# A transformer layer on one core: the last chunk's attention rows divided with features on the partitions

## The reference

```
h = layernorm(x) * (1 + ca) + sa
q, k, v = h Wq.T + bq, h Wk.T + bk, h Wv.T + bv      # 16 heads of 8 features
scores = q k.T / sqrt(8) * exp(-alpha |i - j|)
out = softmax(scores) v                               # the division of this case
x = x + ga * (out Wo.T + bo)
h = layernorm(x) * (1 + cb) + sb
x = x + gb * (shared(h) + sum over the 2 best of 16 experts of p_e * expert_e(h))
```

## Time and profile before

| what | value |
|---|---|
| median of 3 runs | 241.84 us (241.4 to 242.19) |
| the profiled execution | 241.85 us |
| its span, first to last instruction | 240.1 us |
| TensorE busy | 226.1 us, 94% |
| VectorE busy | 190.9 us, 80% |
| GpSimd busy | 190.2 us, 79% |
| ScalarE busy | 163.3 us, 68% |
| first matmul of the expert stage | 156.08 us |

### The profile page before, as it was taken

How to read it: one execution, slowest core, us unless ns; L and a number is a source line. 1 busy time by engine, 2 the same in 40 slices (tenths; PEclk the granted TensorE clock), 3 DMA queues, 4 the chain that set the end, 5 groups by cost and what they waited for, 6 DMA issues and landing times.

```text
span 240.1 us, 5810 instructions
## 1 busy us (share of the span) xinstructions
PE 226.1 (94%) x1830; PEld 167.3 (70%) x1830; DVE 190.9 (80%) x791; ACT 163.3 (68%) x321; POOL 190.2 (79%) x345
## 2 busy tenths in 40 slices
PE   7997999998999998999999899999999999999994
PEld 7775567665567676557677567677888888688882
DVE  3599788896998889999979988468756886976763
ACT  4447867777867799867887678586657658565550
POOL 6489988999999999997999999618486644676661
PEclk9999999999999999999999999999999999999998
DMA  5717814742006632005734450015323340026211
GB/s 140 222 33 175 282 76 96 200 114 79 0 4 141 191 85 72 0 4 127 201 71 139 165 191 3 3 45 147 108 76 125 122 131 3 0 102 197 104 44 44
DMA packets 16302, 24.38 MB, mean 102 GB/s; under 512 B 3280, under 2 KB 5968, under 8 KB 16144
## 3 DMA queue, kind: packets, MB, share of 16 engines
q1 hardware_dynamic: 15840, 24.01, 34.4%
q10 hardware_dynamic: 432, 0.01, 0.1%
HBM read 13.39 MB, written 1.18 MB: 61 GB/s over the span
## 4 chain that ended last, share of the span: by engine, by line
PE 41%; POOL 39%; DVE 12%; ACT 3%; issue 3%; DVEq 0%; ACTq 0%
PE bank L916 41%; POOL sc L298 34%; DVE sc L711 4%; POOL rstd L271 3%; POOL wgu_sb L307 1%; DVE sc L880 1%; DVE attn_t L634 1%; DVE qk L626 1%; DVE qk_st L808 1%; ACT xn L372 1%; POOL nmr L276 1%; DVE mx L711 1%; POOL nmean L269 1%; ACT L575 1%; DVE cw L703 1%
## 5 line engine op out<-in xcount | busy, mean ns | idle before, releaser
L298 POOL TENSOR_SCALAR sc<-sc,mx 128x256 f32<-128x256 f32 x256 | 122.2, 495 | 4.2 <-DVE mx L711 4.1
L711 DVE CUSTOM_DVE_ANT_0 sc<-bank,decay 128x256 f32<-128x256 f32 x256 | 91.0, 418 | 13.6 <-PE bank L916 13.4
L405 ACT ACTIVATE pr<-bank 128x512 f32<-128x512 f32 x128 | 69.4, 595 | 23.2 <-PE bank L916 23.1
L916 PE MATMUL bank<-id_f,sc 128*128 128x128 f32 x512 | 69.9, 278 | 4.0 <-ACT pr L405 1.9
L347 POOL TENSOR_TENSOR act_lo<-sc,act_hi 128x512 fp32r<-128x512 f32 x35 | 45.2, 1296 | 33.0 <-ACT act_hi L566 33.0
L916 PEld LDWEIGHTS bank<-id_f,sc 128*128 128x128 f32 x512 | 55.8, 141 | 18.7 <-issue 8.7
L916 PE MATMUL bank<-pr,v_one 128*32 128x256 f32 x512 | 34.3, 385 | 0.0
L874 DVE TENSOR_TENSOR pr<-bank,cwb 128x512 f32<-128x512 f32 x32 | 22.0, 687 | 14.3 <-PE bank L916 14.0
L575 ACT ACTIVATE bank<-bank 128x512 f32<-128x512 f32 x32 | 18.6, 582 | 19.0 <-PE bank L916 18.7
L880 DVE TENSOR_TENSOR sc<-pr,bank 128x512 f32<-128x512 f32 x36 | 24.7, 687 | 5.8 <-ACT bank L575 2.6
L916 PE MATMUL bank<-h_hi,wgu_hi 128*128 128x512 f32 x72 | 28.5, 395 | 0.0
(11 more groups left out here) (108 smaller groups left out, 274.9 us busy)
## 6 DMA issues: line engine op xcount, KB each, us to landing
cwb<-cw_dram SPq DMA_DIRECT2D x64, 128.0 KB, 3.0
qk_st<-qk SPq DMA_DIRECT2D x60, 128.0 KB, 2.7
wgu_sb<-in_w_gu SPq DMA_DIRECT2D x1, 1152.0 KB, 5.6
wgu_sb<-in_x_t SPq DMA_DIRECT2D x4, 256.0 KB, 3.5
x_all<-in_x SPq DMA_DIRECT2D x1, 768.0 KB, 6.9
o_sum<-o_t SPq DMA_DIRECT2D x6, 128.0 KB, 2.3
o_val<-o_t SPq DMA_DIRECT2D x6, 128.0 KB, 2.2
out_dram<-wgu_sb SPq DMA_DIRECT2D x3, 256.0 KB, 3.3
```

The source lines that it names most:

```text
L298: last = nc.gpsimd.tensor_scalar(sc[:, n % RING, t, :], sc[:, n % RING, t, :], -1.0, mx[:, n % RING, t:t + 1], ALU.mult, ALU.add)
L405: nc.scalar.activation(pr[:, n % RING, :, :].rearrange("p a b -> p (a b)"), turn_bank(i, n)[:], ACT.Exp, scale=-1.0).then_inc(s["exp_done" ...
L711: last = nc.vector.tensor_tensor_reduce(sc[:, n % RING, t, :], ps_s[n % SB][:, t * SEQ:t * SEQ + SEQ], decay[:, t, :], float(HD) ** -0.5, ...
L916: return nc.tensor.matmul(o, l, r, start=start, stop=stop, skip_group_check=not check, is_transpose=transpose or None)
```

## The change

Chunk 3 is divided as chunks 0 to 2 are: `move_rows(3, k)` on SyncE, behind `weights_out(1)`, and one multiply `norm(3)`. The inverse is taken not by ScalarE's Ln and Exp, but by VectorE's reciprocal on o_sum in place, in four pieces of 128 x 128, between units 2, 3 (two pieces) and 4. `by_token`, `norm_tokens`, `attn_turn` and `attn_take` go. The steps behind the division move: `project_o` and `residual` from u = 4 to 5, `res_turn` and `x2_take` from 5 to 6, the statistics from 6 to 7, the root from behind the split of 7 to that of 8; `weights_turn(2)` goes ahead, from 6 to 3.

```diff
@@ SyncE
             weights_out(1)
+            for k in range(2):
+                move_rows(NCHUNK - 1, k)
@@ GpSimd
-                    if i == 0 and u == 7:
+                    if i == 0 and u == 8:
                         ln2_root(NCHUNK - 1)
                         ln2_shift(NCHUNK - 1)
@@ ScalarE
-                        if u == 3:
-                            attn_take(c)
-                        if u == 5:
+                            weights_take(c - 1)
+                        if u == 6:
                             x2_take(c)
-                        if u == 6:
-                            weights_take(c - 1)
@@ VectorE
-            def norm_tokens(k):
...
+            def inverse_piece(t):
+                if t == 0:
+                    for k in range(2):
+                        dve.wait_ge(s_sums[k], 16 * NCHUNK)
+                at = slice(t * P, t * P + P)
+                last = nc.vector.reciprocal(o_sum[:, at], o_sum[:, at])
+                if t == TT - 1:
+                    last.then_inc(s["rec_ok"], 1)
...
-                    if q == 6:
-                        norm_tokens(0)
...
-                        if u == 1:
-                            norm_tokens(1)
+                        for t in {2: (0,), 3: (1, 2), 4: (3,)}.get(u, ()):
+                            inverse_piece(t)
                         if u == 4:
+                            norm(c)
+                        if u == 5:
                             residual(c)
-                        if u == 6:
+                        if u == 7:
                             dve.wait_ge(s["x2_ok"], c + 1)
@@ TensorE
-                        pe.wait_ge(s["cwt_ok"], i - 1)
-                        by_token(i, 0)
...
-                        pe.wait_ge(s["token_ok"], 1)
+                        pe.wait_ge(s["cwt_ok"], i - 1)
                         ln2t(i - 1)
...
-                        if u == 1:
+                        if u == 3:
                             pe.wait_ge(s["lg_ok"], c)
-                            by_token(c, 1)
-                        if u == 3:
-                            attn_turn(c)
-                        if u == 4:
+                            weights_turn(c - 1)
+                        if u == 5:
+                            pe.wait_ge(s["cwt_ok"], c)
                             project_o(c)
-                        if u == 5:
+                        if u == 6:
                             res_turn(c)
-                        if u == 6:
-                            pe.wait_ge(s["x2_ok"], c + 1)
-                            weights_turn(c - 1)
```

More of the change, by code:

```diff
@@ L104, in build @@
         o_t = sb("o_t", [P, 2, CHUNK])
-        rsum = sb("rsum", [P, TT * QUAD, 2])
-        attn = sb("attn", [P, TT * QUAD, 2, HD, 2])
         o_val, o_sum = sb("o_val", [P, CHUNK]), sb("o_sum", [P, CHUNK])
@@ L129, in build @@
             "stats_ok mv_ok vare_ok rstd_ok nmean_ok nmr_ok xn_ok lnt_done h_ok qk_mm qk_hi_ok qk_lo_ok v_mm v_ok "
-            "s_done ttr_done nd_done t_done exp_done pv_done ot_ok c_done rs_ok token_ok ln_ok rec_ok norm_ok "
-            "at_done at_ok wo_done rt_ok rx_done x2_ok stats2_ok mv2_ok vare2_ok rstd2_ok nmean2_ok nmr2_ok xn2_ok ln2t_done "
+            "s_done ttr_done nd_done t_done exp_done pv_done ot_ok ln_ok rec_ok norm_ok "
+            "wo_done rt_ok rx_done x2_ok stats2_ok mv2_ok vare2_ok rstd2_ok nmean2_ok nmr2_ok xn2_ok ln2t_done "
             "h2t_ok h2hi_ok h2lo_ok r_done lg_ok top_ok fill_ok ls_ok struck_ok ex_ok zs_ok rz_ok em_ok "
@@ L413, in inverse_sums @@
                 nc.scalar.activation(o_sum[:], o_sum[:], ACT.Exp, scale=-1.0).then_inc(s["rec_ok"], 1)
-            def attn_take(c):
-                act_e.wait_ge(s["at_done"], 1)
-                nc.scalar.activation(attn_t[:], ps_m[:], ACT.Copy).then_inc(s["at_ok"], 1)
             def x2_take(c):
@@ L739, in early @@
                     qk_lo_of(i + 1, 0, ps_m)
-                if i == NCHUNK - 1:
-                    if q == 3:
-                        norm(i - 1)
-                    if q == 6:
-                        norm_tokens(0)
+                if i == NCHUNK - 1 and q == 3:
+                    norm(i - 1)
             def late(i, q):
@@ L984, in values @@
                 last.then_inc(s["pv_done"], 1)
[L986 to L992, removed]
             def project_o(c):
[L995 to L998, removed]
+                pe.wait_ge(s["norm_ok"], c + 1)
                 mm(ps_m[:], wa_sb[:, W_O, :], attn_t[:]).then_inc(s["wo_done"], 1)
@@ L1025, in early @@
                     lnt(1)
[L1026 to L1030, removed]
-                        pe.wait_ge(s["cwt_ok"], i - 1)
-                        by_token(i, 0)
+                if q == 6 and i and nxt:
+                    pe.wait_ge(s["qk_lo_ok"], 2 * i + 4)
+                    res_turn(i - 1)
             def middle(i, q):
@@ L1207, in _ @@
                     if i == 0:
-                        if u == 1:
+                        if u == 3:
                             pe.wait_ge(s["lg_ok"], c)
-                            by_token(c, 1)
-                        if u == 3:
-                            attn_turn(c)
-                        if u == 4:
+                            weights_turn(c - 1)
+                        if u == 5:
+                            pe.wait_ge(s["cwt_ok"], c)
                             project_o(c)
-                        if u == 5:
+                        if u == 6:
                             res_turn(c)
-                        if u == 6:
-                            pe.wait_ge(s["x2_ok"], c + 1)
-                            weights_turn(c - 1)
                     if i == 1:
                         if u == 3:
-                            pe.wait_ge(s["cwt_ok"], c)
+                            pe.wait_ge(s["x2_ok"], c + 1)
                             ln2t(c)
```

## The result

The changed kernel takes 247.97 us (median of 6 runs, 247.45 to 249.44) against 241.72 us before (6 runs): ratio 1.0266, 95% interval 1.0239 to 1.0294. The forecast was 247.4 us, slower.

The account below looks back on a forecast made before the run. GpSimd was taken to bound the kernel until 153 us, then TensorE, with VectorE lacking slack in units 1 to 4. Terms -0.88 + 4.2 + 0.5 = +3.8, plus 1.8 for the clock, gave 247.4 us, range 244.7 to 249.1.

Parts of the forecast that it names:

- two groups of transposes in the experts: Expert stage, TensorE: removing the transposes of o_t's second half and of attn saves 0.44 us a group, -0.88 us.
- half 0's transposes in the attention: Last attention chunk: four transposes of o_t's first half and the VectorE pair behind lie in GpSimd's stretch, worth 0.
- stall at the projection: Expert stage, behind unit 5: TensorE waits for VectorE's multiply into attn_t from 166.8 to 171.0 us, +4.2 us.
- half clock behind it: TensorE's clock falls to half inside the new stall and slows the matmuls of unit 6: +1.8 us.
- later nmr: Layer norm one unit later: GpSimd's root delays unit 12's second half by +0.5 us (0 to 1.0).
- The reciprocal's price: VectorE's RECIPROCAL on 128x128, in no row: 0.94 us a piece from the slope of the 4- and 32-element rows.
- The stall's size: From VectorE's queue: multiply could start at 169.27, is held by GpSimd's split, ends near 170.9; +4.2 us.
- The clock: TensorE's clock falls in the 4.2 us stall, +1.8 us; rival with clock held, 245.6 us, chance 0.33.
- bounds of 0 and 2.5: Clock loss: 0 if raised on return, 2.5 us for half rate over 5 us, from matmuls at the kernel's start.
- VectorE or TensorE work taken out before 153 us is hidden under GpSimd and worth nothing: Last attention chunk: the chain lies on GpSimd's negated differences from 142.47 us, so removals there count 0.

Follow-up runs that it names:

- e5: Kernel before, with the division of the first half of o_t left out of the last attention chunk: 241.74 us against 242.44, ratio 0.9978.
- e4: Changed kernel with the inverse left out except for one column of o_sum: 242.82 us, ratio 1.0059 to the kernel before.
- e1: Changed kernel with 17 useless 512-column matmuls added ahead of the projection's wait: 245.72 us, ratio 1.0183 to the kernel before.
- e2: Changed kernel with GpSimd's root of the last layer norm back behind the split of unit 7: 247.48 us, ratio 1.0249 to the kernel before.
- e6: Changed kernel with the removed tensors rsum and attn (2176 bytes a partition) still allocated: 248.95 us, ratio 1.0270 to the kernel before.
- e12: Kernel before with rsum and attn allocated behind act_lo, same instructions: 242.23 us against 241.60, ratio 1.0030.
- e13: Changed kernel with only rsum (128 bytes a partition) still allocated: 249.06 us, one run.
- e14: Changed kernel with only attn (2048 bytes a partition) still allocated: 249.34 us, one run.
- e3: Changed kernel with the last inverse piece and the multiply ahead of unit 4's second product: 246.30 us, ratio 1.0229 to the kernel before.
- e7: Changed kernel with one inverse piece in each of units 2 to 5, projection in unit 7, later steps moved back: 243.74 us against 242.44, ratio 1.0064.
- e10: Changed kernel with rsum and attn still allocated, inverse pieces in units 2 to 5, projection in unit 8: 242.53 us against 241.60, ratio 1.0037.

## Why the prediction was right

By its steps, in span time:

| term | forecast | measured | from |
|---|---|---|---|
| two groups of transposes in the experts | -0.88 | about -0.9 | lag at units 0, 5 and 7, without the moved steps |
| half 0's transposes in the attention | 0 | -0.43 | changed kernel, e5 |
| stall at the projection | +4.2 | +4.17 | timeline, e4 |
| half clock behind it | +1.8 | +1.61 | timeline, e1 |
| later nmr | +0.5 | +0.56 | lag at unit 12, e2 |
| slower pace of all later matmuls | none | about +1.0 | e6, e12, e13, e14 |
| shorter wait for the router weights | none | -0.25 | lag at unit 24, e12 |
| sum | +5.6 | +5.8 | span: +5.8 |

- **The reciprocal's price** was the line through two rows, 0.94 us; it is 0.94. The Trainium skill's repeat count of 8 ("VectorE: DVE Perf Modes", section on the 8-slice pipeline in each mode), taken as 8 cycles an element, would have given 1.2 by the estimate in the prediction; the trace doesn't agree.
- **The stall's size** came from laying VectorE's queue out operation by operation. The multiply was forecast to be held by the split and to end 1.6 us after it could start; it took 1.55, and e3 shows 0.69 with GpSimd idle. The Trainium skill's exclusive lock ("SBUF — State Buffer", on the port pair that VectorE shares with GpSimd) would end it 0.69 after the split, at 170.60; it ended at 170.45.
- **The clock** was the step with least behind it, a fall seen only after the last matmul, and its size owes something to luck. e1 shows the cause. The loss is 1.61 us: projection, three down products and one gate matmul take 3.47 us from 170.61 to 174.08, where they take 1.86 at the full rate in the kernel before. The forecast's 1.8 was a choice between bounds of 0 and 2.5. The 2.5 came from durations at the start of the kernel before, where its trace has the granted clock at full in every microsecond, so no row shows it. And the loss is no fixed number: the stretch at half rate was 3.4 us in four traces (the changed kernel, e2, e3, e13) and 6.8 in two (e6, e14), and there it cost 1.1 to 1.2 us more, beyond the upper bound. The fall did not come 2.0 us after the last matmul, as at the end of the kernel before, but 4.1 us after TensorE ran dry, when it was about to start again. The Trainium skill ("TensorE: Matmul & The Clock Gate", section on the clock gate) has it that the throttled state is the default and activity lifts it. The trace agrees in so far as the clock came back at 174.0 while TensorE worked; no trace here shows the low clock at the start, before the first matmul.
- **What failed.** "VectorE or TensorE work taken out before 153 us is hidden under GpSimd and worth nothing" is wrong by 0.43 us. The forecast took the engine that the chain named for the bound. e5 shows that a loop through TensorE and ScalarE's exponential set the pace there: with GpSimd's run unchanged, the transposes behind it came 0.43 us earlier, and the chain of the kernel after runs through TensorE and ScalarE. And the forecast, which priced removed instructions, had no term for removed allocations; their slower pace costs about 1.0 us and shortens the wait for the router weights by 0.25. The three terms that were not forecast come to +0.3 us: they nearly cancel, which is luck too.
- **What stays open.** Why 128 bytes change the matmuls' pace by 2%, and which of the tensors behind o_val does it. When the half-rate stretch is the long one. It doesn't go with the pace: e6 and e13 both have the fast one, and e6 has the long stretch, e13 the short one. In the two traces with the long one the clock had fallen 0.8 and 1.2 us before TensorE started again, in the four others between 0.1 us before and 0.5 us after that; whether this is the reason was not tested. Both long ones are traces from the second chip, as is the short one of e13; whether the chip plays a part isn't shown. The longest execution of the changed kernel (249.44 us, mean clock 0.985 against 0.992) may have had the long stretch or, as e13 (0.986), a second fall elsewhere. And one untraced execution each of e4, e7, e10 and e12 has a mean clock of 0.992 or 0.993 and is about 1.3 us above its median, which would fit one fall of 3.4 us that the traces of these kernels don't show.

## What to carry to other kernels

Before moving a step from TensorE to an engine that is "80% busy", lay out that engine's queue at the very place and see when the result is there; a step that saves TensorE 0.9 us can make it wait for 4. A wait of a few microseconds on TensorE can cost more than its length, since the clock may fall and the matmuls behind run at half rate; where the wait can't be avoided, independent matmuls in the gap gave that part back here, though they were useless. A chain through a trace names one releaser at each step, the last that the profile sees: before work is called hidden under it, check in the trace whether another engine releases the same step at the same time. And when tensors are removed or added, compare the pace of unchanged matmuls first, or the layout's effect is taken for the edit's.

## What the runs showed of the hardware

- RECIPROCAL on VectorE costs 6.1 ns per further element of a partition: 0.18 us for 4, 0.35 for 32, 0.94 for 128.
- A VectorE product with both inputs in SBUF (128x512) took 0.69 us with GpSimd idle (e3) and 1.55 to 1.58 beside its split (the changed kernel, e7, e10); reciprocals beside it kept their length of 0.94.
- The granted clock fell to half in stalls of about 4 us, and after one of 2.4 us just when TensorE had come back (e3), but not in the traces with waits of 1.2 us (e7, e10). In e13 it fell once more in the attention, behind waits of 0.67 us at most.
- The stretch at half clock lasted 3.4 us in five cases and 6.8 in two.
- The pace of 512-column matmuls in units without an extra step was 0.227 or 0.231 us at the same full clock. It was 0.227 with the tensors from o_val to act_lo 128 or 2176 bytes further on than in the changed kernel, and 0.231 with them 0 or 2048 bytes further on.
